# Maxima across partitions by a diagonal and a product, low halves of x on GpSimd, and a turned loop, in a conditional adapter layer with a mixture of experts

## The reference

```
H      = x @ W.T                                   # 512 -> 512
xc     = H + ((x @ A[idx].T) @ Bm[idx].T) * scalings[idx]
shared = sum over 2 experts of gelu(xc @ Wsh_up) @ Wsh_down     # 512 -> 256 -> 512
probs  = softmax(xc @ W_router); the two largest give the gates
routed = sum over 2 chosen of 16: gate * (gelu(xc @ Wrt_up) @ Wrt_down)
out    = x + shared + routed
```

## Time and profile before

| | us |
|---|---|
| median of three executions | 745.32 (742.05 to 746.18) |
| the profiled execution | 750.71 |
| its span (first to last instruction) | 748.7 |
| PE busy | 667.6 (89%) |
| DVE busy | 455.2 (61%) |
| ACT busy | 327.6 (44%) |
| POOL busy | 225.8 (30%) |

### The profile page before, as it was taken

The page is one execution under the profiler, slowest core; times in us unless marked ns, Lnnn a source line. Parts: engine busy times, 40 slices in busy tenths (PEclk is TensorE's granted clock), DMA queues, the critical chain, the costliest instruction groups (busy, mean ns, idle before and its releaser), DMA issues.

```text
span 748.7 us, 13753 instructions
## 1 busy us (share of the span) xinstructions
PE 667.6 (89%) x4116; PEld 438.1 (59%) x4117; DVE 455.2 (61%) x900; ACT 327.6 (44%) x480; POOL 225.8 (30%) x288
## 2 busy tenths in 40 slices
PE   5998998878878878788899999999999999999895
PEld 2556555544544745555666666666666667656462
DVE  2778998655556289853444544444454453688775
ACT  1242325444445656256455555545455554333230
POOL 1000000000000236247333333333333322777772
PEclk9998998878879899799999999999999999999998
DMA  6779963222212424216555455555555545999967
GB/s 256 301 266 320 397 239 110 98 90 87 85 56 84 140 90 141 85 33 218 159 155 151 141 148 155 146 143 148 157 142 147 159 127 213 375 310 353 369 201 255
DMA packets 49764, 135.67 MB, mean 181 GB/s; under 512 B 6160, under 2 KB 6288, under 8 KB 47312
## 3 DMA queue, kind: packets, MB, share of 16 engines
q1 hardware_dynamic: 38304, 97.93, 35.6%
q0 software_dynamic: 11440, 37.50, 18.4%
HBM read 86.38 MB, written 49.02 MB: 181 GB/s over the span
## 4 chain that ended last, share of the span: by engine, by line
PE 47%; DVE 17%; POOL 11%; issue 10%; DMA 8%; ACT 4%; SPq 0%; ACTq 0%; POOLq 0%; DVEq 0%
PE bank L1395 13%; PE bank L1414 13%; POOL rtw L608 8%; PE bank L1379 4%; PE bank L1259 4%; DMA act_in<-xT 4%; DVE lot_max L908 4%; PE bank L1276 3%; PE bank L1404 3%; PE bank L1329 2%; DVE rtw L937 2%; PE bank L1251 2%; DVE x_max L949 2%; ACT rtw L641 1%; DMA region<-xc_dram,slot_idx 1%
## 5 line engine op out<-in xcount | busy, mean ns | idle before, releaser
L1131 DVE SCALAR_TENSOR_TENSOR region<-bank,scale,region 128x512 f16<-128x512 f32 x79 | 59.2, 751 | 132.2 <-ACT region L811 132.2
L1395 PE MATMUL bank<-rtw,region 128*128 x948 | 117.3, 273 | 0.0
L1414 PE MATMUL bank<-rtw,tmp 128*128 x474 | 115.2, 379 | 0.3 <-DVE tmp L1139 0.3
L1395 PEld LDWEIGHTS bank<-rtw,region 128*128 128x128 f16 x948 | 89.3, 98 | 15.5 <-issue 1.5
L1329 PE MATMUL bank<-act_in,shw 128*128 128x256 f16 x768 | 91.5, 280 | 6.2 <-POOL act_in L542 4.0
L1342 PE MATMUL bank<-shw,hid 128*128 128x512 f16 x384 | 88.9, 390 | 8.1 <-DVE rtw L1195 4.6
L574 POOL DMA_INDIRECT region<-xc_dram,slot_idx x79 | 77.1, 976 | 61.3 <-POOL slot_idx L571 61.3
L1329 PEld LDWEIGHTS bank<-act_in,shw 128*128 128x128 f16 x768 | 76.4, 101 | 20.8 <-POOL act_in L542 4.6
L608 POOL DMA_INDIRECT rtw<-r_dram,row_idx x64 | 72.4, 1130 | 27.3 <-issue 18.6
L818 ACT ACTIVATE region<-bank,un_dn 128x512 f32<-128x512 f32 x79 | 54.3, 687 | 57.5 <-PE bank L1414 53.7
L807 ACT ACTIVATE tmp<-bank,un_up 128x256 f32<-128x256 f32 x79 | 37.4, 473 | 80.3 <-PE bank L1395 80.3
(11 more groups left out here) (158 smaller groups left out, 943.9 us busy)
## 6 DMA issues: line engine op xcount, KB each, us to landing
r_dram<-region SPq DMA_DIRECT2D x79, 256.0 KB
rtw<-rt_w SPq DMA_DIRECT2D x16, 1024.0 KB, 7.5
act_in<-xT SPq DMA_DIRECT2D x16, 512.0 KB, 4.2
xc_dram<-rows SPq DMA_DIRECT2D x16, 512.0 KB, 5.0
xcT_dram<-hid SPq DMA_DIRECT2D x16, 512.0 KB, 2.9
rtw<-x_rows SPq DMA_DIRECT2D x16, 512.0 KB, 4.5
rtw<-xcT_dram SPq DMA_DIRECT2D x13, 512.0 KB
out<-rtw SPq DMA_DIRECT2D x9, 512.0 KB
```

The costliest lines, as they stand in the source:

```text
L1131: nc.vector.scalar_tensor_tensor(xgT[s][:, 1], R_XT[s][:].rearrange("p (k t) -> p k t", k=HK), col(scale, C_ALL).bitcast(F32), xgT[s][:, 0 ...
L1395: last = mm(R_UP[s][:, 0:D], xgT[s][:, xp, k, :], rtw[:, bass.ds(e, 1), w0:w0 + D].rearrange("p a d -> p (a d)"), start=(k == 0 and n == 0 ...
L1414: last = mm(R_DN[s][:], midT[s][:, xp, m, :], rtw[:, bass.ds(e, 1), w0:w0 + H].rearrange("p a h -> p (a h)"), start=(m == 0 and n == 0), s ...
```

## The change

1. **Maxima across partitions.** The partial maximum in each partition is cut to its power of two. DVE multiplies the identity by it, which makes a diagonal in bfloat16 (`x_diag`, `diag`; a power of two is exact there). PE multiplies a matrix of ones by it (`spread_x`, `spread`), so that each partition holds the row of all 128, in a corner of the logits' PSUM bank (`SPREAD`). DVE takes the maximum of that row. The product for x of chunk c+2 stands ahead of `router_products(c-1)` and shares its signal. The trip of the last maximum through DRAM goes.
2. **Low halves of x.** `x_low` leaves DVE. ACT, after the high half, scales `act_in` in place as well; POOL subtracts (`low_x`).
3. **Order on ACT** in the splitting stage: `high_x(c+1)`, `cond_T(c-1)`, four L641, `cond_rows(c)`. On DVE both `low_routed` stand ahead of `x_scales`, and in the search stage all lots do.
4. **The first steps** of the adapted layer are written out anew on PE and DVE; the maxima of the shared weights are searched later.
5. **The routed loop is turned**: its body is now `r_down(j)`, `r_transpose_mid(j+1)`, `r_up(j+2)`, `r_transpose_x(j+4)`, and the register load, of four numbers instead of three, stands ahead of `r_down`.

```diff
+            def low_x(c, s):                        # POOL
+                pool.wait_ge(x_half, c - 1)
+                nc.gpsimd.tensor_tensor(un_cond[s][:], x_unscale[s][:].bitcast(F32), col(unscale, LIN_W).bitcast(F32), ALU.mult)
+                nc.gpsimd.tensor_tensor(xp[s][:, 1], act_in[s][:], xp[s][:, 0], ALU.subtract).then_inc(x_split, 1)
...
                 nc.scalar.activation(xp[s][:, 0], act_in[s][:], ACT.Copy, scale=x_scale[s][:].bitcast(F32))
+                nc.scalar.activation(act_in[s][:], act_in[s][:], ACT.Copy, scale=x_scale[s][:].bitcast(F32)).then_inc(x_half, 1)
...
+            def routed_step(i, s, more=True):       # ACT
+                c = 2 * i + s
+                if more:
+                    high_x(c + 1, 1 - s)
+                cond_T(c - 1, i - 1 + s, 1 - s)
+                for e in range(2):
+                    high_routed(2 * c - NC + e)
+                if not more:
+                    high_condT(0, 0, C_EARLY, early=True)
+                cond_rows(i, s)
...
+                dve.wait_ge(x_max_ready, 2 * i + s - 1)         # end of x_largest
+                nc.vector.tensor_scalar(x_diag, ident[:], x_max[s][:], None, ALU.mult).then_inc(x_diag_ready, 1)
...
             def x_scales(c, s):
-                dve.wait_ge(x_reduced, c - 1)
+                if c < 4:
+                    dve.wait_ge(spread_ready, c)
+                else:
+                    dve.wait_ge(logit_ready, c - 2)
+                nc.vector.tensor_reduce(x_max_all[s][:], SPREAD[:, 2, :], AX_X, ALU.max).then_inc(x_all_found, 1)
...
                 low_routed(2 * c - NC)
+                low_routed(2 * c - NC + 1)
                 if more:
                     x_scales(c + 2, s)
-                low_routed(2 * c - NC + 1)
...
+            def spread_x(c):                        # PE
+                pe.wait_ge(x_diag_ready, c - 1)
+                return mm(SPREAD[:, 2, :], ones[:], x_diag, start=True, stop=True)
...
+                if peaks_of is not None:            # in router_products
+                    pe.wait_ge(x_all_found, peaks_of - 2)
+                    spread_x(peaks_of)
...
-            def r_pair(i, first=False, more=True):
+            def r_round(i, first=False):
                 e = r_experts(i)
                 for s in range(2):
                     j = 2 * i + s
-                    r_transpose_mid(j, s, first and i == 0)
-                    r_up(j + 1, 1 - s, e[s + 1], first and i == 0 and s == 0)
-                    if more:
-                        r_transpose_x(j + 3, i + 1 + s, 1 - s)
-                    if first and i == 0 and s == 0:
-                        pe.wait_ge(shared_ready, NT * EARLY)
-                    r_down(j, s, e[s], first and i == 0)
+                    r_down(j, s, e[s], first)
+                    r_transpose_mid(j + 1, 1 - s, first and s == 0)
+                    r_up(j + 2, s, e[2 + s])
+                    r_transpose_x(j + 4, i + 2, s)
```

More of the change, by code:

```diff
@@ L739, in _ @@
             for s in range(2):
[L740 to L746 removed]
+                routed_step(A_HALF - 1, s, more=s == 0)
             cond_T(NC - 1, A_HALF - 1, 1)
@@ L1268, in cond_transposes, with spread, router_products @@
                     last.then_inc(xpose_ready, 1)
-            def router_products(c, s, first=False):
+            def spread_x(c):
+                pe.wait_ge(x_diag_ready, c - 1)
+                return mm(SPREAD[:, 2, :], ones[:], x_diag, start=True, stop=True)
+            def spread(n, m):
+                pe.wait_ge(diag_ready, n)
+                for k in range(m):
+                    last = mm(SPREAD[:, k, :], ones[:], x_diag if n == 4 else diag[k], start=True, stop=True)
+                return last
+            def router_products(c, s, peaks_of=None, first=False):
                 pe.wait_ge(condT_ready, NT * c + NT)
-                if not first:
+                if first:
+                    pe.wait_ge(x_all_found, 1)
+                else:
                     pe.wait_ge(logit_copied, c)
+                    pe.wait_ge(all_found, 2)
+                if peaks_of is not None:
+                    pe.wait_ge(x_all_found, peaks_of - 2)
+                    spread_x(peaks_of)
                 for t in range(NT):
```

219 lines of the change are left out of this document (125 added, 94 removed).

## The result

| | before | after |
|---|---|---|
| median, us | 745.75 (742.05 to 749.36, 4 runs) | 690.45 (689.18 to 695.04, 4 runs) |
| profiled execution, us | 750.71 | 690.69 |
| its span, us | 748.7 | 688.6 |
| TensorE's granted clock | 0.940 | 0.962 |

The account below looks back on a forecast made before the run. PE was nearly full except in the splitting stage, where it waited in a ring with ACT and DVE at a lowered clock. Terms -40 +1 -1 -6 = -46 took 750.7 to 704.7, the median 745.3 to 699; range 681 to 720.

Parts of the forecast that it names:

- Splitting stage: Steps 9 to 15: PE no longer waits for ACT's copy; 11.4 us a step, 82 against 122.4, 40 us less.
- the slack that I kept for slips: Splitting stage: 0.8 to 1.5 us spare everywhere in a step, which was taken at 11.4 us.
- the operations without a row: DVE's new diagonal and maximum of 128 numbers, not in the trace: 0.3 us taken, bounds 0.15 and 0.6 each.
- Routed rounds: Moving the register load ahead of the down products saves 0.15 us a pair: 6 us less, bounds 21 less, 10 more.
- the rival of a more exposed load: Routed rounds: four numbers and short products ahead raise 0.55 to 0.8 us; 10 us more, total 715; chance 0.06.
- the routed stall goes entirely: Routed rounds: the register load is hidden as the lead grows; 15 us more saved than counted, total 684; chance 0.12.
- the carrying over of 5.4 us: Whole kernel: the profiled execution's 5.4 us above the median before was assumed to hold after the change too.
- The start: Start and search stage: later weight loads and PE held longer while x arrives late; 1 us more, bounds -4 to +8.
- Sorting: Without the DRAM trip the third shared input comes sooner, but PE waits for DVE; 1 us less.
- The ring of the shared port: Splitting stage: POOL's subtraction and DVE's lows hold each other; 19.5 us a step, median 755; slower, chance 0.04.
- The late part and the clock: Late part untouched, 0, bounds 2 us each way; PE's clock in the splitting stage over 0.95.

## Why the prediction came out as it did

*Splitting stage: right, the size 3 us too small.* The mechanism is shown from both sides, by the order alone and by all but the order on ACT. Steps took 10.98 us, PE's own work, not 11.4; the slack that I kept for slips was not used, and only 2 us stayed at the end. Of the operations without a row, both small ones came out at 0.28, as taken, but the diagonal took 0.69 where POOL's subtraction ran; the subtraction took 2.13.

*Routed rounds: the step that failed.* The term said 6 us less, and 21.7 were measured. It rested on how far PE's sequencer is ahead when it comes to the load: "I take 0.15 saved a pair", out of bounds of 0.02 to 1.18 us. In the loads shown above the lead is 0.8 us before (368.0 to 368.79) and 0.95 after (381.7 to 382.65), so the place gave what I took. What I had wrong is the load itself. I let "one more number is loaded" count as a cost, without a row, and gave it as a reason for the rival of a more exposed load; in the traces the load of four numbers takes 0.33 us where that of three takes 0.95. By the estimate above this removes the stall. It was to be read before: the trace of the kernel before has the load of three numbers at 0.77 to 1.05 us, where I only said that 2.2 us pass for down's issue and the load together. The rival "the routed stall goes entirely", to which I gave 0.12, had the size right, and gave the longer lead as its reason. That the time still fell into the range was luck in part: the start and the carrying over of 5.4 us went the other way. The Trainium skill, "DMA: Bandwidth & Descriptors", section "Latency and other measured facts", gives a floor of about 600 ns for a register load. The traces do not agree: 0.33 us for four numbers lies below it.

*The start: +1 said, +4.8 measured, inside the bounds of -4 to +8, and the reason named only by half.* That PE is held longer while x arrives late was right as a description and wrong as a cause: letting PE go earlier brought nothing in either of two runs. The traces show a chain by way of DVE and SP instead, which explains a part. The maxima of the shared weights are searched at 29.77 now, in a busy stretch, where they stood at 18.81 in one with idle time. The first weight lot is searched at 38.16 instead of 34.00; SP, which waits for it, issues the next weights at 40.47 instead of 36.30; the load of x for chunk 4 stands behind them, at 44.49 instead of 41.37; and DVE's x maximum, once at 49.64, is at 51.50. DVE in the kernel before:

```profile
18.81 2.29 DVE L1001 TENSOR_REDUCE largest<-rtw 128x1 f32<-128x2048 f32 x1 [1.95 <-DMA rtw<-sh_dn]
...
34.00 2.28 DVE L908 TENSOR_REDUCE lot_max<-rtw 128x2 f32<-128x2048 f32 x1
```

DVE in the changed kernel:

```profile
29.77 2.27 DVE L1006 TENSOR_REDUCE largest<-rtw 128x1 f32<-128x2048 f32 x1
...
38.16 2.28 DVE L894 TENSOR_REDUCE lot_max<-rtw 128x2 f32<-128x2048 f32 x1
...
51.50 1.22 DVE L946 TENSOR_REDUCE x_max<-act_in 128x1 f32<-128x1024 f32 x1 [5.97 <-DMA act_in<-xT]
...
113.89 1.22 DVE L946 TENSOR_REDUCE x_max<-act_in 128x1 f32<-128x1024 f32 x1 [3.19 <-DMA act_in<-xT]
...
124.14 2.05 DVE L918 TENSOR_SCALAR unscale<-neg_expo 128x3 int32<-128x3 int32 x1
```

SP's queue before:

```profile
36.30 5.02 SPq L376 DMA_DIRECT2D rtw<-rt_w  x2
41.37 0.43 SPq L359 DMA_DIRECT2D act_in<-xT  x1
```

and now:

```profile
40.47 3.98 SPq L378 DMA_DIRECT2D rtw<-rt_w  x2
44.49 0.43 SPq L361 DMA_DIRECT2D act_in<-xT  x1
```

No run moved that search alone, so this chain is read from two traces and not shown. It makes DVE 1.9 us late at 51.50, of which 0.9 is left at x's maximum of step 6 (101.3 against 100.4). The rest comes in steps 7 and 8, mostly from the two last rows of DVE: it waits 3.19 us for x, where it waited for nothing before, and an operation on 128x3 numbers takes 2.05 us beside POOL's subtraction (124.03 to 126.16). In the second execution of the same program DVE does not wait there, that operation takes 0.17, and step 9 starts at 131.6 instead of 133.6. The kernel before varies too: with the turned loop, which changes nothing ahead of the rounds, its step 9 starts at 125.7 instead of 128.8. So the 4.8 us of one pair of profiles are good to some 3 us.

That the parts other than the order (diagonals, subtractions, the first steps written anew and the later search) together cost 10 to 16 us before step 9 is shown: with the same order on ACT and DVE, step 9 starts at 119.9 and 121.3 in the two kernels without diagonals, and at 131.6 to 135.9 in the five that have them and the order as changed (the changed kernel twice, with the old loop twice, with x's low half on DVE). The last of these has no subtractions, and x's low half on DVE in their place, so which part costs how much is open. The 4.8 us of the table is 12.3 of this (133.6 less 121.3), less 7.5 that the new order wins up to step 9 (128.8 less 121.3), most of it in step 8, which it shortens from 16.3 to 10.9 us; I had counted the order from step 9 only.

*Sorting: -1 said, +0.1 measured.* Both sides came: the third shared input is no longer late, and PE waits for DVE instead, once for 5.6 us. DVE is held by POOL's subtractions about as often as before, at other links of its chain, such as this cast, which takes 0.17 alone:

```profile
223.94 2.06 DVE L881 CAST chosen<-best_i_c 128x4 f32<-128x4 uint32 x1
```

Over all kernels of the study, the five without the change in this stage took 90.3 to 94.7 us, 92.7 in the mean, and the nine with it 88.1 to 91.6, 89.9 in the mean. So it is worth some 3 us by these means, which the one pair of profiles does not show.

*The ring of the shared port: did not come here, but its rule shows in a run.* In the step shown of the splitting stage of the changed kernel the subtraction and the weight lows do not meet. In the kernel with the maximum back on POOL they do, at 199.20, as its POOL rows above say; DVE there:

```profile
196.70 2.48 DVE L946 SCALAR_TENSOR_TENSOR rtw<-rtw,scale 128x1024 f16<-128x1024 f32 x2 [0.32 <-ACT rtw L640]
199.42 4.17 DVE L946 SCALAR_TENSOR_TENSOR rtw<-rtw,scale 128x1024 f16<-128x1024 f32 x2 [0.24 <-ACT rtw L640]
```

The two parts that meet it take 4.17 us instead of 2.48. That is what the Trainium skill, "SBUF — State Buffer", section "SBUF: two separate sides", says of an operation with two SBUF inputs beside a GpSimd one.

*The late part and the clock* were as forecast: 125.8 against 125.7, and a clock of 1.00 between 133.56 and 212.43. That the late part agrees to 0.1 us is chance, since it varies by 6 us between executions of one program (122.8 and 129.3 above).

## What to carry to other kernels

When engines wait for one another in a ring, look first at the order within the queues: a new order of the same statements on ACT and DVE alone brought 48 us here, where the whole change brought 55. Order and turned loop without the rest were 1.8% faster than the whole change, so the diagonals, the work moved to POOL and the first steps written anew cost time together; which of them does is not separated. Before a load of registers is moved, read from the trace how long it takes: here it was three times as long with three numbers as with four, and an edit that changes place and number at once does not tell which of them counts. An idle engine isn't free for any work: before giving GpSimd a second kind of operation, look in the trace for what it pays at the change of kind, and before removing a wait of PE, find out whether the engine that releases it is the one that paces the stage.

## What the runs showed of the hardware that was not expected

- GpSimd stands some 7 us (5.7 to 12.0 in two runs), in gaps put down to "issue", whenever it goes from the maximum across partitions to an elementwise operation or back; one tiny operation a step cost 56 us that way. The Trainium skill, "GPSIMD Engine Reference", section "Instruction dispatch", gives about 6 us for the first call to a freshly loaded kernel of GpSimd's, with no instruction to be seen in the profile. The gaps are of this size and mostly 1 us longer; here the queue shows two instructions MODIFY_POOL_CONFIG at each change, and that code is loaded each time is not shown. It also means that the change could not have moved x's low halves to POOL and left the maxima there: its parts 1 and 2 belong together.
- A 128x128 diagonal on DVE takes 0.28 us, the maximum of a row of 128 in PSUM 0.28, and the 128x128 product of ones and diagonal occupies PE for 0.06 between its neighbours.
- A load of three register numbers on PE takes 0.94 to 0.95 us in the median (0.77 to 1.05) and one of four 0.33 (0.33 to 0.82), in five kernels and in nine.
